# Staging buffers loaded one slab ahead in the projections of layer 1, and alternating load semaphores in a projection of layer 0

## The reference

```
x = layernorm(x + quaternion_attention(x))     # layer 0: q, k, v, o are quaternion-linear; full softmax, 16 heads of 64
x = layernorm(x + quantized_linear(x))         # layer 0: x and W rounded to blocks of 32 on a 6-bit grid
x = layernorm(x + window_attention(x))         # layer 1: 16 query heads, 2 key/value heads, window 256
x = layernorm(x + sigmoid(xr @ Wr.T) * (relu(xk @ Wk.T)**2 @ Wv.T))   # xr, xk: mixes of a token and the one before
```

## Time and profile before

| | us |
|---|---|
| median of three runs | 5428.95 |
| the profiled execution | 5435.68 |
| its span (core 2, the slowest; the cores take 5405.0 to 5434.1) | 5434.1 |
| PE busy with matmuls in it | 2720.7 |
| ACT busy | 1807.2 |
| DVE busy | 1533.8 |

### The profile page before, as it was taken

How to read it: one execution, slowest core, us unless ns; L and a number is a source line. 1 busy time by engine, 2 the same in 40 slices (tenths; PEclk the granted TensorE clock), 3 DMA queues, 4 the chain that set the end, 5 groups by cost and what they waited for, 6 DMA issues and landing times.

```text
span 5434.1 us, 62675 instructions; the slowest of 8 cores (5405.0 to 5434.1 us)
## 1 busy us (share of the span) xinstructions
PE 2720.7 (50%) x17729; PEld 1393.0 (26%) x17810; DVE 1533.8 (28%) x3379; ACT 1807.2 (33%) x2292; POOL 177.8 (3%) x339
## 2 busy tenths in 40 slices
PE   0255157777776424355555556463255555514434
PEld 0122113444443112132232323231022222202112
DVE  0355310000000123422223232324143333323554
ACT  0022106777774024254544445350022222201000
POOL 0011010000000100000000000000100000000000
PEclk9977676666666755556666666666656666657767
DMA  1332130000001310000000000000401111131000
GB/s 16 70 39 35 40 47 9 4 4 4 4 4 19 55 35 12 23 12 11 13 11 16 11 16 10 18 7 23 79 24 30 30 30 29 29 54 31 20 28 24
DMA packets 193866, 132.70 MB, mean 24 GB/s; under 512 B 123752, under 2 KB 174608, under 8 KB 193552
## 3 DMA queue, kind: packets, MB, share of 16 engines
q0 software_dynamic: 46864, 59.31, 6.6%
q1 hardware_dynamic: 146688, 69.38, 4.8%
HBM read 117.63 MB, written 28.31 MB: 27 GB/s over the span
## 4 chain that ended last, share of the span: by engine, by line
PE 34%; ACT 23%; DVE 17%; DMA 9%; issue 9%; SPq 5%; POOL 1%; DVEq 1%; ACTq 1%; PEldq 0%; POOLq 0%
ACT TE L521 18%; PE PALL L551 10%; PE PALL L509 4%; PE PALL L464 3%; PE PALL L332 2%; PE PALL L1262 2%; PE PALL L797 2%; DMA TY<-XFF 2%; PE PALL L1194 1%; PE PALL L1407 1%; PE PALL L1467 1%; DMA SMALL<-QBI 1%; DVE TE L1246 1%; ACT TE L1238 1%; PE PALL L718 1%
## 5 line engine op out<-in xcount | busy, mean ns | idle before, releaser
L521 ACT ACTIVATE TE<-PALL,BIASB 128x768 bf16<-128x768 f32 x1536 | 1383.6, 901 | 971.0 <-PE PALL L509 592.0
L509 PE MATMUL PALL<-TY 64*128 64x384 bf16 x3072 | 863.6, 423 | 698.0 <-ACT TE L521 686.2
L509 PEld LDWEIGHTS PALL<-TY 64*128 64x128 bf16 x3072 | 302.7, 99 | 1205.3 <-issue 1128.3
L551 PE MATMUL PALL<-TY,TE 128*128 128x65 bf16 x9216 | 530.6, 243 | 0.0
L551 PEld LDWEIGHTS PALL<-TY,TE 128*128 128x128 bf16 x9216 | 503.1, 131 | 59.9 <-issue 59.9
L558 DVE RECIPROCAL SMALL<-PALL 128x6 f32<-128x6 f32 x48 | 9.4, 196 | 1643.6 <-PE PALL L551 1617.0
L332 PE MATMUL PALL<-TY,TE 128*128 128x512 bf16 (+1 forms) x817 | 203.6, 411 | 382.3 <-DVE TE L298 216.7
L1238 ACT ACTIVATE TE<-PALL,BIASB 128x256 bf16<-128x256 f32 (+2 forms) x240 | 154.6, 644 | 464.8 <-PE PALL L1223 445.0
L464 PE MATMUL PALL<-TE,TY 128*128 128x512 bf16 x500 | 148.1, 446 | 245.4 <-DMA TY<-XFF 244.7
L332 PEld LDWEIGHTS PALL<-TY,TE 128*128 128x128 bf16 x832 | 86.7, 106 | 499.0 <-issue 427.9
L718 PE MATMUL PALL<-TE,TY 128*128 128x512 bf16 x271 | 86.2, 468 | 198.4 <-DMA TY<-ATT 124.9
(11 more groups left out here) (171 smaller groups left out, 2597.1 us busy)
## 6 DMA issues: line engine op xcount, KB each, us to landing
TY<-XFF POOLq DMA_DIRECT2D x192, 128.0 KB, 5.0
TY<-XST POOLq DMA_DIRECT2D x18, 512.0 KB, 3.7
YOUT<-TE SPq DMA_DIRECT2D x18, 512.0 KB, 2.6
ATT<-TY SPq DMA_DIRECT2D x36, 128.0 KB, 1.8
Y2SP<-TY SPq DMA_DIRECT2D x18, 256.0 KB, 2.0
TE<-Y2SP POOLq DMA_DIRECT2D x18, 256.0 KB, 2.9
ATT<-TY SPq DMA_DIRECT2D x18, 256.0 KB, 2.3
Y3SP<-TY SPq DMA_DIRECT2D x18, 256.0 KB, 2.0
```

What stands on the lines that cost most here:

```text
L509: t.matmul(o_, l_, r_, start=True, stop=True, tile_position=tp)),
L521: ss.activation(o_, i_, AF.Exp, bias=BIASB[:, 63:64], scale=0.125)),
L551: t.matmul(o_, l_, r_, start=s0, stop=False, skip_group_check=True)),
```

## The change

Three edits are made.

1. In `emit_p1b` the eight loads of a block raise the semaphores `db` and `dx0` in turn, the second load carries the same waits as the first, and PE's first matmul of each group waits for both. Buffer and order stay.
2. In the K/V projection YSTG becomes two buffers (bytes 16384 and 24576 of TY3). The loads of slabs 0 and 1 are written before the loop, and those of slab si+2 behind the matmuls of slab si, whose `nop` they wait for.
3. In the Q projection the same two buffers are used. The loads of tiles 0 and 1 are written before the loop, and those of tile qt+2 right behind the Q matmuls of tile qt and a new `nop`. So on SP they now stand ahead of the spills of tile qt.

```diff
             for blk in range(8):
...
                 for ic in range(8):
-                    tld = sch.dma("g", "db",
+                    sem = "db" if ic % 2 == 0 else "dx0"
+                    t_ = sch.dma("g", sem,
...
-                                  waits=wt if ic == 0 else [])
+                                 waits=wt if ic < 2 else [])
...
-                            w = [tld]
+                            w = [tld0, tld1]
...
-        def YSTG(ic, n):
-            return TY3V(16384, BF16, 8 * 512)[:, ic * 512: ic * 512 + n]
+        def YSTG(pb, ic, n):
+            return TY3V(16384 + pb * 8192, BF16, 8 * 512)[:, ic * 512: ic * 512 + n]
...
+        def emit_kv_cast(si, extra=()):
             n = 512 if si < 4 else 256
-            dls = "dl0" if si % 2 == 0 else "dl1"
+            pb = si % 2
+            dls = "dl0" if pb == 0 else "dl1"
...
-                    w = [("dy2", 16 * NSL), tp2_nop, p2v_last]
-                    if ystg_free:
-                        w.append(ystg_free)
+                    w = [("dy2", 16 * NSL), tp2_nop, p2v_last] + list(extra)
...
+        emit_kv_cast(0)
+        emit_kv_cast(1)
+        for si in range(5):
...
-            ystg_free = sch.op("t", lambda t: t.nop(), mark=True)
+            ystg_free[pb] = sch.op("t", lambda t: t.nop(), mark=True)
+            if si + 2 < 5:
+                emit_kv_cast(si + 2, extra=[ystg_free[pb]])
...
+        def emit_q_cast(qt, extra=()):
+            pb = qt % 2
+            dls = "dl0" if pb == 0 else "dl1"
...
+        emit_q_cast(0, [ystg_free[0], vt_done])
+        emit_q_cast(1, [ystg_free[1], vt_done])
         for qt in range(NQT):
-            qcast = None
-            for ic in range(8):
-                w = []
-                if ic == 0:
-                    w = [ystg_free, vt_done] + ([prev_q_t] if prev_q_t else [])
...
+            qcast = q_cast[qt]
...
-            prev_q_t = q_ready
+            qfree[qt] = sch.op("t", lambda t: t.nop(), mark=True)
+            if qt + 2 < NQT:
+                emit_q_cast(qt + 2, [qfree[qt]])
```

More of the change, by code:

```diff
@@ L442, in emit_p1b @@
                 wt = list(first_waits) + ([xsg2_free] if xsg2_free else [])
-                tld = None
+                tld0 = tld1 = None
                 for ic in range(8):
-                    tld = sch.dma("g", "db",
-                                  (lambda gg, s_=XFF[128 * ic:128 * ic + 128, 512 * blk:512 * blk + 512],
-                                   d_=XSG2(ic, 0, 512): gg.dma_start(out=d_, in_=s_)),
-                                  waits=wt if ic == 0 else [])
+                    sem = "db" if ic % 2 == 0 else "dx0"
+                    t_ = sch.dma("g", sem,
+                                 (lambda gg, s_=XFF[128 * ic:128 * ic + 128, 512 * blk:512 * blk + 512],
+                                  d_=XSG2(ic, 0, 512): gg.dma_start(out=d_, in_=s_)),
+                                 waits=wt if ic < 2 else [])
+                    if ic % 2 == 0:
+                        tld0 = t_
+                    else:
+                        tld1 = t_
+                tld = tld0
                 for sub4 in range(4):
@@ L986, in build_program @@
         z5 = sch.op("v", lambda v: v.memset(V1T3[:, :, 64:65], 1.0))
-        def YSTG(ic, n):
-            return TY3V(16384, BF16, 8 * 512)[:, ic * 512: ic * 512 + n]
+        def YSTG(pb, ic, n):
+            return TY3V(16384 + pb * 8192, BF16, 8 * 512)[:, ic * 512: ic * 512 + n]
         kv_done = None
-        ystg_free = None
-        for si in range(5):
+        ystg_free = {0: None, 1: None}
+        kv_cast = {}
+        def emit_kv_cast(si, extra=()):
             n = 512 if si < 4 else 256
-            dls = "dl0" if si % 2 == 0 else "dl1"
+            pb = si % 2
+            dls = "dl0" if pb == 0 else "dl1"
             cast_tok = None
@@ L999, in build_program @@
                 if ic == 0:
-                    w = [("dy2", 16 * NSL), tp2_nop, p2v_last]
-                    if ystg_free:
-                        w.append(ystg_free)
-                cast_tok = sch.dma("y", dls, (lambda y, d_=YSTG(ic, n),
+                    w = [("dy2", 16 * NSL), tp2_nop, p2v_last] + list(extra)
+                cast_tok = sch.dma("y", dls, (lambda y, d_=YSTG(pb, ic, n),
                                               s_=Y2SP[512 * si:512 * si + n,
@@ L1007, in build_program @@
                                    waits=w)
+            kv_cast[si] = cast_tok
+        emit_kv_cast(0)
+        emit_kv_cast(1)
+        for si in range(5):
+            n = 512 if si < 4 else 256
+            pb = si % 2
             for which in (0, 1):
@@ L1014, in build_program @@
                     if ic == 0:
-                        w = [l_wv1, l_b1v, cast_tok]
+                        w = [l_wv1, l_b1v, kv_cast[si]]
                         if psum_free.get(bank):
@@ L1019, in build_program @@
                                         l_=TY3V(woff, BF16, 8 * 128)[:, ic * 128:(ic + 1) * 128],
-                                        r_=YSTG(ic, n),
+                                        r_=YSTG(pb, ic, n),
                                         s0=(ic == 0), s1=(ic == 7):
@@ L1167, in build_program @@
                "b6_free": None, "atm_free": None, "expt_free": None}
-        prev_q_t = None
-        for qt in range(NQT):
-            qcast = None
-            for ic in range(8):
-                w = []
-                if ic == 0:
-                    w = [ystg_free, vt_done] + ([prev_q_t] if prev_q_t else [])
[L1175 to L1179, removed]
+        q_cast = {}
+        def emit_q_cast(qt, extra=()):
+            pb = qt % 2
+            dls = "dl0" if pb == 0 else "dl1"
+            tok = None
+            for ic in range(8):
+                w = list(extra) if ic == 0 else []
+                tok = sch.dma("y", dls, (lambda y, d_=YSTG(pb, ic, QT),
+                                         s_=Y2SP[qt * QT:(qt + 1) * QT,
+                                                 128 * ic:128 * ic + 128]:
+                                         y.dma_start_transpose(d_, s_)),
+                              waits=w)
+            q_cast[qt] = tok
+        emit_q_cast(0, [ystg_free[0], vt_done])
+        emit_q_cast(1, [ystg_free[1], vt_done])
+        qfree = {}
+        for qt in range(NQT):
+            qcast = q_cast[qt]
             q_marks = []
@@ L1191, in build_program @@
                                         l_=TY3V(0, BF16, 8 * D)[:, ic * D + oc * 128: ic * D + oc * 128 + 128],
-                                        r_=YSTG(ic, QT),
+                                        r_=YSTG(qt % 2, ic, QT),
                                         s0=(ic == 0), s1=(ic == 7):
```

## The result

The changed kernel takes 5338.0 us (median of 8 runs, 5324.8 to 5355.3); the kernel before takes 5428.9 us in the same series (8 runs). The ratio is 0.9833, with a 95% interval of 0.9818 to 0.9849: 82 to 99 us less. The profiled execution fell from 5435.7 to 5336.0 us. The forecast was 5328 us, with a range of 5312 to 5340: the measured time lies inside the range, 2 us from its upper end, and above the 5322 to 5334 that had 60 in 100.

A forecast was written before the change was run, and what follows sets the result against it. No engine was busy over half the span, so each stage was read by what PE waits for. Terms -30.0 - 72.3 + 0.8 = -101.5 us, from 5428.95, gave 5328 us; range 5312 to 5340 for 8 in 10.

The forecast's parts named there:

- K/V projection: -30 forecast: Layer 1: with a second buffer SP issues transpose groups without a hole; -30 us, bounds -27 and -31.
- Q projection: -72.3 forecast: Layer 1: early loads at five tile boundaries leave PE waiting for DVE's LayerNorm; -72.3 us, bounds -70 and -81.5.
- one boundary in five at full speed: Q projection: four boundaries counted at 14.0 us with the clock low, one at 16.3 with the clock kept.
- V projection of layer 0: +0.8 forecast: Alternating semaphores on one buffer remove no wait; added waits cost 0.05 us x 16, bounds 0 and +4.
- rival B: The small end: group 1 dragged by W1O, clock low at all boundaries, double wait paid; -93, 5336 us; 15 in 100.
- the double wait: Layer-0 V projection: PE waits for two semaphore counts at each group; at most 3.8 us, +4 in the small end.
- W1O's drag: K/V projection: the weight load W1O delays group 1 until group 0 has landed; everything 4 us later, -27 left.
- A: Q boundaries: the clock stays up in the shorter idle time; -110.7, 5318 us; 20 in 100.
- C: Q loads not hidden: something ahead on SP keeps them until the tile's end, only K/V gains; about 5400 us; 2 in 100.
- D: SP becomes the bound: early Q transposes issue so slowly that attention's spills slip; about 5465 us; 3 in 100.
- two halves: Skill page on DMA: all issuers share 16 engines; issuing is usually small beside transfer, else K/V would gain only 20 us.

The follow-up runs named there:

- the kernel with four banks: The changed kernel with the Q blocks in PSUM banks 0 to 3 in turn, not in 0 and 1 alone: 5317.7 us, ratio 0.9773.
- the first experiments: Four kernels on one chip: first edit alone (ratio 1.0004), changed kernel without it (0.9838), two buffers in K/V alone (0.9944) or Q alone (0.9882).

## Why the prediction came out as it did

*K/V projection: -30 forecast, -28.4 measured.* The mechanism was as described. The term was 1.6 us too large, and the working behind it, which gave 31.2, by 2.8. The greater part of that is in the chain of waits after (start, us, what), which answers to the earlier trace rows:

```profile
...
3849.46 6.41 SPq L1013
...
3860.69 1.47 SPq L1013
...
3862.20 3.09 SPq L1013
...
3865.49 1.12 SPq L1013
...
3866.67 1.25 SPq L1013
...
```

I had let the eighth issue of group 0 take 1.25 us; it took 3.09, beside the tail of W1O. So group 1 began 2.5 us before PE's first matmul and not 4.2: 1.7 us. I could have read it before: in the earlier trace rows that issue and its landing took 5.32 us together where an undisturbed one took 2.35. Another 0.6 us came because three groups take 10.5 to 10.9 us each from start to start, and not 10.35. With W1O held back the issues took 1.3 us each, which shows the cause of the first part.

*Q projection: -72.3 forecast, -69.5 measured,* 13.9 us a boundary. A boundary after, PE, DVE and SP, which answers to the earlier trace rows:

```profile
...
4158.35 0.50 PE L1130 MATMUL PALL<-ROWR,ONER 1*128 1x512 f32 x1
...
4158.78 2.77 PE L1218 MATMUL PALL<-TY 128*128 128x384 bf16 x16
...
4165.59 0.81 DVE L1165 TENSOR_SCALAR TY<-TE,SMALL 128x1024 bf16<-128x1024 f32 x1 [0.98 <-ACT SMALL L1160]
4166.51 1.34 DVE L1222 TENSOR_SCALAR TY<-PALL,BIASB 128x384 bf16<-128x384 f32 x2
...
4167.38 10.70 PE L1218 MATMUL PALL<-TY 128*128 128x384 bf16 x48 [5.83 <-DVE TY L1222]
...
4178.26 0.62 DVE L1222 TENSOR_SCALAR TY<-PALL,BIASB 128x384 bf16<-128x384 f32 x1 [0.68 <-PEq L1227]
...
```

PE goes on with Q as soon as the slice's last matmul has streamed, does two blocks in 2.8 us, and stands 5.83 us (5.7 forecast) until DVE, done with the LayerNorm at 4166.40, has evicted the first block. The last eviction begins 11.9 us after that LayerNorm; before it was 25.3. These are 13.4 us of the 14.0 that I had for a boundary at the low level: the six blocks behind the gap take 10.7 us and not 10.2. (The remaining 0.3 to 0.5 us of the 13.9 lie in the attention between two boundaries; what gives them is not shown.) The part of the term that was most off is the clock: I had counted one boundary in five at full speed, 2.3 us more. The same stretch by engine, with the granted clock in the third column from the end:

```profile
...
4163.00:4168.00 5.00, 0.62 (x3) 0.31 (x4) 2.52 (x6) 1.65 (x4) 0.00 (x0) 0.81 0.30 101
4168.00:4173.00 5.00, 5.00 (x17) 2.33 (x16) 0.78 (x2) 0.00 (x0) 0.00 (x0) 0.50 0.01 4
4173.00:4178.00 5.00, 5.00 (x31) 2.83 (x29) 2.30 (x4) 0.00 (x0) 0.00 (x0) 1.00 0.00 0
...
```

In this gap the clock held at first, but it went to the low level 1.3 us before PE came back (the mean of 0.81 over 4163 to 4168 puts the fall near 4166.1) and stayed there to 4173, so PE ran slow for 5.6 us after a gap of 5.8. At all five boundaries the last 48 matmuls take 10.5 to 10.7 us; at full speed they would take 7.8. So the low level cost 2.7 to 2.9 us a boundary. The Trainium skill's rule ("TensorE: Matmul & The Clock Gate", section "HAM oscillation — how this bites in real kernels"), that work after a long enough wait starts at half rate, held for this gap; after the 3.1 to 3.5 us gaps of the kernel with four banks it held at some and not at others.

*V projection of layer 0: +0.8 forecast,* nothing that the runs could tell from zero measured.

*From the profile to the time.* My sum of -101.5 stands against 97.9 us in the two stretches and 99.7 us in the times of the profiled executions. The forecast of 5328 is nevertheless 10 us below the median, since I took the sum from the median of three runs, 5428.95. In the 17 runs of the first experiments the kernel before takes 5432.0, 13.5 us above its median core; the changed kernel takes 5338.0, 17.3 above its own. By these numbers 3.7 of the 10.5 us are the sum, 3.0 the base and 3.8 that the slowest core stands farther from the median core. The first is shown by the stretches. The other two are only a bookkeeping: the median of the kernel before is 5428.9 in the changed kernel's own series, and the distance of the slowest core moves between 12 and 19 us from one kernel to the next here, without an order that these runs explain. I added nothing for either, and that the time still fell inside the range is owed to the range's width. The time came near rival B's 5336, whose reasons hold only in part: the clock was low at all boundaries, but the double wait cost nothing and W1O's drag was 1.7 us of the 4.

*Rivals.* A falls by the rows above. C falls: only the first Q load ends a wait of PE. D is answered by SP's queue after, which answers to the earlier trace rows:

```profile
...
4178.32 10.80 SPq L1195 DMA_TRANSPOSE TY<-Y2SP  x8
4198.21 0.33 SPq L1173 DMA_DIRECT2D Y3SP<-TY  x1
4254.78 1.30 SPq L1318 DMA_DIRECT2D ATT<-TY  x3
...
```

The group of tile qt+2 takes 10.8 us here (single transposes at most 2.30 us). It ends 9 us before the slice spill at 4198.21 and 66 us before the spills of the attention result.

*The Trainium skill's page "DMA: Bandwidth & Descriptors"* (section "Issuing engines are not separate DMA queues") had two halves in my working. Its first half, that DMAs of all issuers share the engines, fits what four kernels show, though none of them shows the sharing itself: transposes on SP take 1.3 us to issue alone and up to 5.5 to 7 us beside W1O or W1Q from POOL. Its second half, that issuing is usually small beside the transfer, does not hold for this kernel's transposes: a group issues for 10.4 us, and its last transpose lands 2.35 to 2.7 us after its issue began.

## What to carry to other kernels

A second staging buffer pays the time that lies between "buffer free" and "data landed", where the loads really move forward in their queue, and as far as the issuing queue keeps up: in the K/V projection PE's gaps fell from 12 us to 4, because a group takes SP 10.5 us to issue. Renaming or splitting semaphores on one buffer moves nothing. When a wait is taken away, read on every in-order engine what stands ahead of the next step: here DVE's LayerNorm took over at once, and writing the projection ahead of it was worth another 68 us. A load that is put off must go where no other load is needed soon, or its cost only moves.

## What the runs showed of the hardware

- The issue of a transposing DMA on SP's queue takes 1.26 us when little else moves, and up to 6.41 us beside W1O and 7.01 us beside W1Q (eight loads each from POOL, float32 to bf16, 256 KB written by each), so the issuing queue itself stands still and all behind it waits. Beside W1V (32 KB each) it stayed at 1.26 us.
- A gap of 5.8 us of PE was followed by 5.6 us at the 1.2 GHz level, though the clock was still granted in full through the first 4.6 us of the gap; after gaps of 3.1 to 3.5 us the next 32 matmuls ran at the 2.4 GHz level at three boundaries (5.36 us) and partly at the low level at two (6.63 and 8.19 us). So a part of the price of such a gap is paid behind it: 2.9 us of longer matmuls (10.7 us for 7.8) on top of the 5.8 us.
